# A two-layer fused kernel: scores, outer products, B, statistics and row sums in other places, and layer zero's residual added by VectorE instead of GpSimd

## What is computed

```
xn = layernorm(x)
s  = retention(xn)            # scores = (q k^T) * gamma^(i-j), causal; s = scores v
g  = silu(ffn0(xn))           # h = silu(w1)*w2 ("z"), gelu(h1), gelu(h2), w3
x  = x + s * g                # layer zero's residual
xn = layernorm(x)
s  = s6(xn)                   # in-projection, causal convolution of 4 taps, silu; B, C;
                              # h[t] = A h[t-1] + x[t] B[t], y = C h + D x, gated, out-projection
r  = score of each token; the 512 highest of 1024 get  sigmoid(r) * ffn1(xn)  added to xn
x  = x + s * silu(that sum)
```

## Time and profile before

| | us |
|---|---|
| runs | 546.86, 544.11, 549.14; median 546.86 |
| the profiled execution | 545.56 |
| its span, first to last instruction | 543.8 |

### The profile page before, as it was taken

The page is one execution under the profiler, slowest core; times in us unless marked ns, Lnnn a source line. Parts: engine busy times, 40 slices in busy tenths (PEclk is TensorE's granted clock), DMA queues, the critical chain, the costliest instruction groups (busy, mean ns, idle before and its releaser), DMA issues.

```text
span 543.8 us, 6040 instructions
## 1 busy us (share of the span) xinstructions
PE 443.4 (82%) x1777; PEld 259.0 (48%) x1791; DVE 407.9 (75%) x659; ACT 291.4 (54%) x475; POOL 404.7 (74%) x316
## 2 busy tenths in 40 slices
PE   0796978898889897989899888989798999485743
PEld 0575645644564455545565456445554464131211
DVE  2282144959788977989598959898789779958985
ACT  3664736774567545763676366745676447313300
POOL 1673543887599959985999769985999599855582
PEclk9997979899999999999999999999999999978865
DMA  8300006311513143221532162214321332215220
GB/s 316 136 20 4 1 0 175 85 51 40 155 60 86 50 125 108 77 77 47 152 96 78 37 176 77 79 39 118 115 79 58 96 99 78 78 44 165 85 74 19
DMA packets 25379, 46.97 MB, mean 86 GB/s; under 512 B 3072, under 2 KB 4096, under 8 KB 25088
## 3 DMA queue, kind: packets, MB, share of 16 engines
q1 hardware_dynamic: 24336, 45.13, 28.1%
q10 hardware_dynamic: 1008, 1.41, 0.8%
HBM read 42.33 MB, written 4.19 MB: 86 GB/s over the span
## 4 chain that ended last, share of the span: by engine, by line
POOL 35%; DVE 23%; issue 17%; PE 16%; ACT 5%; DMA 1%; SPq 0%; DVEq 0%; POOLq 0%; ACTq 0%
POOL hs L548 15%; DVE hs L1359 10%; PE bank0a L932 7%; DVE xbank L1336 7%; POOL hidAl L510 6%; POOL hidBl L510 5%; PE bank1a L1012 2%; POOL xnTl L492 2%; POOL g L526 2%; POOL g L522 2%; DMA Bt<-w_in 1%; POOL xr L530 1%; POOL q L499 1%; PE ybank L1071 1%; DVE st L1262 1%
## 5 line engine op out<-in xcount | busy, mean ns | idle before, releaser
L548 POOL TENSOR_TENSOR hs<-hs,Ct 128x512 f32<-128x512 f32 x127 | 184.6, 1459 | 32.6 <-DVE hs L1359 19.7
L510 POOL TENSOR_TENSOR hidAl<-plain,hidAh 128x512 fp32r<-128x512 f32 x48 | 64.6, 1346 | 37.7 <-ACT hidAh L643 31.3
L1359 DVE TENSOR_TENSOR_SCAN hs<-decay,carry,xbank 128x512 f32<-128x512 f32 x63 | 80.5, 1278 | 7.6
L510 POOL TENSOR_TENSOR hidBl<-plain,hidBh 128x512 fp32r<-128x512 f32 x48 | 66.1, 1378 | 26.6 <-ACT hidBh L643 18.7
L1359 DVE TENSOR_TENSOR_SCAN hs<-decay,xbank 128x512 f32<-128x512 f32 x64 | 78.0, 1219 | 5.6 <-DVE xbank L1336 0.5
L1336 DVE TENSOR_TENSOR xbank<-xs,bbank 128x512 f32<-128x512 f32 x104 | 71.4, 687 | 1.3
L642 ACT ACTIVATE plain<-bank0a,col 128x512 f32<-128x512 f32 x64 | 44.2, 690 | 45.2 <-PE bank0a L932 44.0
L932 PE MATMUL bank0a<-hidBh,hTh 128*128 128x512 f32 x128 | 57.7, 451 | 1.7 <-ACT q L675 1.7
L932 PE MATMUL bank0a<-hidAh,hTh 128*128 128x512 f32 x128 | 57.0, 445 | 1.7 <-ACT q L675 1.7
L932 PE MATMUL bank0a<-hidAl,hTh 128*128 128x512 f32 x128 | 51.6, 403 | 0.0
L932 PE MATMUL bank0a<-hidBl,hTh 128*128 128x512 f32 x128 | 50.7, 396 | 0.0
(11 more groups left out here) (184 smaller groups left out, 951.7 us busy)
## 6 DMA issues: line engine op xcount, KB each, us to landing
xs<-x_rows SPq DMA_DIRECT2D x128, 256.0 KB, 3.4
xt<-x_tok SPq DMA_DIRECT2D x8, 256.0 KB, 4.5
xr<-x_feat SPq DMA_DIRECT2D x8, 256.0 KB, 7.6
x_rows<-xc SPq DMA_DIRECT2D x8, 256.0 KB, 2.0
out<-xr SPq DMA_DIRECT2D x7, 256.0 KB, 2.2
fh<-h_w SPq DMA_DIRECT2D x1, 1024.0 KB, 10.0
hs<-h_w SPq DMA_DIRECT2D x1, 1024.0 KB, 11.9
lw<-l_w ACTq DMA_DIRECT2D x1, 640.0 KB, 5.4
```

Source lines behind the costliest of these rows:

```text
L510: pool.tensor_tensor(low[:, m, :], plain[:, k % NPLAIN, :], high[:, m, :].bitcast(F32), ALU.subtract).then_inc(hidden_low, 1)
L548: pool.tensor_tensor(h, h, Ct[:, hs_(u)], ALU.mult).then_inc(p_ready, 1)
L1359: dve.tensor_tensor_scan(hs[:, i % NSTATES, :], decay[:, gr:gr + 1].broadcast_to([P, HALF]), xbank[:], 0.0 if u % 2 == 0 else carry[:, k:k ...
```

## The change

It has these parts. On PE, `scores` goes from slot 2 to slot 4, behind z2(v, 3); `outer` from slot 4 to slot 5, behind the projection for B; B goes from slot 6 to slot 5, ahead of the gate projection; the last gather of a unit goes from slot 8 to slot 9, behind `retention_out` and `retention_in` (not in the last unit). On DVE, `mask_scores` goes from slot 2 to 4 (behind the last z product), `memory` from 4 to 6, `stats_l0` from 7 to 5, `gate_y` from 9 to 11. On POOL, `rstd_l0` goes from slot 8 to 6, `scale_q` from 5 to 6, and `add_residual` is gone: DVE adds the residual right behind the product, waiting for its own product. ACT takes B ahead of the gate.

The row sums: the comparison of an even unit with the other unit now is four `tensor_scalar` instructions of 128x512, which also write the sum of their row into `counts`. The comparison of an odd unit with the even one is not made: whoever does not win against a token loses to it, so that PE subtracts what the even unit counted (`minus_ones`) or adds the row sums (`counts` times the identity), and the threshold of even units is lower by 512.

```
@@ PE slot
-                        elif s == 2:
+                        elif s == 4:
                             scores(v)
-                        elif s == 4:
-                            outer(v)
...
                         elif s == 5:
-                            project("gate", n, W_IN[:, P:2 * P])
-                        elif s == 6:
                             project_x("B", n, W_B)
+                    if v is not None and s == 5:
+                        outer(v)
+                    if n is not None and s == 5:
+                        project("gate", n, W_IN[:, P:2 * P])
...
-                    if s == 8 and t is not None:
-                        gather_y(t, 3)
...
+                    if t is not None and s == (8 if t == UNITS - 1 else 9):
+                        gather_y(t, 3)
@@ PE rank
-                    pe.wait_ge(beats_ready, r + 1)
-                    pe.matmul(bank1d[:], ones[:], beats[:, r % NBEATS, :], start=(pos == 0),
-                              stop=(pos == CH - 1)).then_inc(l1_dve_full if pos == CH - 1 else ranked, 1)
+                    full = l1_dve_full if pos == CH - 1 else ranked
+                    if u % 2 == 1 and pos >= CPH:
+                        j = pos - CPH
+                        pe.matmul(bank1d[:, ck(j)], counts[:, j:j + 1].broadcast_to([P, P]), ident[:], start=False,
+                                  stop=(pos == CH - 1)).then_inc(full, 1)
+                        return
+                    pe.wait_ge(beats_ready, beats_of(u) + pos + 1)
+                    pe.matmul(bank1d[:], ones[:] if pos < CPH else minus_ones[:], beats[:, r % NBEATS, :],
+                              start=(pos == 0), stop=(pos == CH - 1)).then_inc(full, 1)
@@ DVE residual_l0 (and POOL's add_residual is removed)
                 dve.tensor_tensor(g0[:, hs_(t)], bank0d[:], g0[:, hs_(t)], ALU.mult).then_inc(l0_dve_done, 1)
+                dve.wait_ge(l0_dve_done, done(L0_DVE, ("s", t)))
+                dve.wait_ge(x_feat_in[t % 4], (t // 4 + 1) * 16)
+                dve.tensor_tensor(x_of(t), x_of(t), g0[:, hs_(t)], ALU.add).then_inc(x1_ready, 1)
@@ DVE compare_other
-                dve.tensor_tensor(beats[:, CPH:], row.broadcast_to([P, CPH, HALF]), s_i.broadcast_to([P, CPH, HALF]),
-                                  ALU.is_le if u % 2 else ALU.is_lt).then_inc(beats_ready, CPH)
+                for j, c in enumerate(chunks(u + 1)):
+                    dve.tensor_scalar(beats[:, CPH + j, :], srow[:, hs_(u)], scol[:, u // 2 % 2, c:c + 1], 0.0, ALU.is_ge,
+                                      ALU.add, accum_out=counts[:, j:j + 1]).then_inc(beats_ready, 1)
@@ DVE slot
-                    if s == 2:
+                    if s == 4:
                         mask_scores(v)
-                    elif s == 4:
+                    elif s == 6:
                         memory(v)
...
-                    if compare_slots(t)[CPH] == s:
+                    if t % 2 == 0 and compare_slots(t)[CPH] == s:
                         compare_other(t)
...
-                    elif t < UNITS - 1 and s == 9:
+                    elif t < UNITS - 1 and s == 11:
                         gate_y(t)
...
-                    if s == 7:
+                    if s == 5:
                         stats_l0(w)
@@ POOL slot
-                if n is not None and s == 0:
-                    add_residual(n)
...
-                if w is not None and s == 8:
+                if w is not None and s == 6:
                     rstd_l0(w)
...
-                if v is not None and s == 5:
+                if v is not None and s == 6:
                     scale_q(v)
```

38 lines of the change are left out of this document (17 added, 21 removed).

## The result

The changed kernel takes 572.9 us in the median (566.9 to 579.2, 4 runs), the kernel before 545.7 beside it: a ratio of 1.040 with a 95% interval of 1.030 to 1.050. That ratio goes by the two faster executions alone (566.9 and 569.4 us), because the other two (576.4, the one profiled here, and 579.2 us) lie over 1.5% above the fastest. A second set (e_after) gave 571.2 us (564.2 to 575.4) and 1.051 (1.044 to 1.058). 554 was predicted, with a range of 545 to 562. So the direction was right, and the size was short by 17 to 19 us. Even the fastest execution of the eight, 564.2 us, lies outside the range.

The account below looks back on a forecast made before the run. A chain through the engines, with POOL's unbroken 30.9 us run, was taken to set the period. Middle periods +8.4, first period +0.3 and tail -0.6 gave +8.1 us on 545.56; the forecast was 554 us, range 545 to 562.

Parts of the forecast that it names:

- What bounds the kernel: Middle periods: a chain through the engines, POOL's unbroken 30.9 us and the part from there to h1(0), sets the period.
- Residual: +0.5: Middle period, up to the convolution: DVE's added residual delays scan, statistics and gather by 0.5 us (0.2 to 0.75).
- Scores behind z2(3): 0: PE ahead of the transposes: scores and mask wait saved there, 2.3 us, come back as a wait; 0 us.
- B and outer products: +1.95: PE between convolution and h1(0): both now stand there, so h1(0) starts later; +1.95 us per middle period.
- scale_q: +1.25: POOL: scaling of q leaves idle time and enters POOL's unbroken run; +1.25 us per middle period.
- Last gather: 0: PE ahead of h2(0): waits go, but POOL still sets the end of h2; 0 us.
- Row sums: -2.05: POOL's pair of weighings: no longer held by DVE's comparison, so POOL gains 2.05 us in every period.
- The sum: Middle period: all terms, with -0.25 for contention, give +1.4 us; six such periods give +8.4.
- -0.6: The tail (unit 7), bound by DVE and a transfer: residual and changed comparisons together give -0.6 us.
- (d): Rival, chance 0.08: PE's longer idle times lower its granted clock, +3.4 us per middle period, about 574; or tensor_scalars hold POOL, 560.
- the clock below 1.0 in the middle: Sign that the forecast is wrong: PE's granted clock falls below 1.0 in the middle periods.
- DVE's wait of 5 us or more at gate_y: Sign that the forecast is right: DVE waits 5 us or more at gate_y.

Follow-up runs that it names:

- e_res: The kernel before with only layer zero's residual moved from POOL to DVE; 555.2 us, ratio 1.020.
- e_sb: The kernel before with only the moves of scores (mask with them), B and outer products (memory with them), prologue apart; 560.3 us, ratio 1.029.
- e_sbf: The kernel before with the moves of scores, B and outer products, plus 8 matmuls of ones ahead of the transposes of yn; 553.3 us, ratio 1.017.
- e_q: The kernel before with only the scaling of q moved behind low h1(0) on POOL; 551.6 us, ratio 1.013.
- e_ga: The kernel before with the row sums and the last gather behind retention, gate_y two slots later; 554.6 us, ratio 1.013.
- e_gast: The kernel before with row sums, later last gather and gate_y, and the next unit's statistics and rstd two slots earlier; 538.3 us, ratio 0.988.
- e_row: The kernel before with only the row sums of the change; 537.8 us, ratio 0.985.
- e_tr: The changed kernel with 8 matmuls of ones that nothing needs ahead of the transposes of yn, units 0 to 6; 558.0 us, ratio 1.026.

## Why the prediction was wrong

**What bounds the kernel.** Right in the main. POOL's unbroken run and the part ahead of h1(0) set the period; residual and scale_q moved the period by what they moved there. The row sums show where it ends: with POOL 2 us faster, PE takes over from h2 on.

**Residual: +0.5.** The mechanism is right. The size was 0.72, the upper bound, since the room that I took off does not exist. Left out was what the longer wait for the mask does to the clock: another 2.3 us over three periods in e_res.

**Scores behind z2(3): 0.** This is the step that failed. I wrote that the 2.3 us "come back as a wait" at the transposes and priced the wait at nothing. The wait came, 2.23 and 2.5 us long, and as a wait it cost nothing: with it filled by useless matmuls the convolution starts 15.2 us behind the residual product, and without, in the one period of e_after in which the clock has not fallen there, just the same. Its cost is what it does to the clock: 1.6 to 2.7 us in each of the five other periods, 9.4 in all. PE's waits in the middle of the kernel before are short pieces between work (1.34, 0.66, 1.28, 0.58 and 0.47 us in the earlier trace rows, none over 1.8). The change made 2.23 and 1.23 us of the first two, with 0.63 us of transposes between. That they stand close together matters too: in e_sb the first is only 1.4 to 1.8 us long, and the clock still fell behind the pair in four periods of six. In the middle, the listed waits of PE add up to 36 us before and 38 after, hardly more; their lengths differ.

**B and outer products: +1.95.** Right in three periods of six (1.89 in e_sbf), a little high in the others (1.6); the whole period grew by 1.45. **scale_q: +1.25.** Right: 1.22 (e_q).

**Last gather: 0.** Wrong by 0.9 us in favour of the change, in company with the statistics (apart from them it costs, e_ga), and unseen in the end, where unit 6's gate_y costs about 1.2 us.

**Row sums: -2.05.** Nearly right together with gather and statistics (e_gast, -1.85), only 1.0 by themselves. The tensor_scalars do not hold POOL: a pair of weighings beside them takes 2.53 us (e_row). The rule of the Trainium skill that I quoted ("SBUF — State Buffer", on who interferes with whom) holds here.

**The sum.** +1.4 us per middle period, and 1.2 measured with the clock kept up (e_tr). Order alone therefore costs 7.2 us over the six. The clock costs 9.4 more in the middle of the profiled execution. In the medians e_tr gains 13 us (571.2 against 558.0), in the profiled executions 6 (564.2 against 558.3). What remains of the 13 us by which e_tr is slower than the kernel before is prologue (4.3 against a profile that was at the short end) and end (1.0, where I had -0.6).

**The rivals.** The case that came true is (d), the granted clock, with 0.08. I had its mechanism, its place within a wait or two and its sign. I priced it with 3.4 us in every period, the convolution at half speed. (Four pairs at the rate that I quoted would make 3.8.) The falls met scores and gather ahead of it, and in five periods of six: 1.6 us on average. What made me give it 0.08 was that the middle of the kernel before stood at 1.00 throughout. But it stood there with no idle piece of PE over 1.8 us, and the change altered just that. The end of the same trace, at 0.83, with waits of 2 to 5 us, was the warning. Of the signs that I named, the clock below 1.0 in the middle came, which I had put under wrong; DVE's wait of 5 us or more at gate_y did not (at most 3.8 us in e_after). With 0.08 on a case worth 574, and the range drawn to leave it out, the range had to miss.

## What to carry to other kernels

A wait of PE that costs nothing on the path can still cost the clock: when an edit makes a wait of PE longer than any before it, or brings two together, price the matmuls behind it at twice their length as well, and give that case the weight of a main forecast. Keep PE busy in such a wait with matmuls that nothing needs, or with real work moved there; here 8 small bf16 matmuls in each middle period brought 9 us back in the middle of the profiled execution, and 13 in the medians. When a bound engine becomes faster, compare when both engines end, not how long their stretches last.
